# Attention scores, rough scores and broadcast maxima as 64x64 tiles, with keys stored without zero blocks

## The chip, the cores and the metric

The kernel runs on one core of a Trainium2 chip. The metric is the device time of one execution in microseconds (us), as the median of several runs. A core has TensorE (matmuls, PE in the profile; its weight loads are PEld), VectorE (DVE), ScalarE (ACT), GpSimd (POOL) and SyncE (SP), which here issues nearly all DMAs. The engines run their own instruction streams and wait for one another by semaphores.

## What is computed

The input is `x` (8 images, 128 channels, 64x64). It is cut into windows of 8x8 = 64 tokens. Only what matters for the change is shown:

```python
def mha(q, k, v, wq, wk, wv, wf, bf):
    qh = (q @ wq).reshape(B, Lq, HEADS, dh)      # 8 heads of 16
    kh = (k @ wk).reshape(B, Lk, HEADS, dh)
    vh = (v @ wv).reshape(B, Lk, HEADS, dh)
    attn = jnp.einsum('bqhd,bkhd->bhqk', qh, kh) * (1.0 / dh ** 0.5)
    attn = jax.nn.softmax(attn, axis=-1)
    o = jnp.einsum('bhqk,bkhd->bqhd', attn, vh).reshape(B, Lq, C)
    return o @ wf + bf
```

There is self-attention inside each window at 64x64, then at 16x16 after a mean over 4x4 pixels, and cross-attention in which each 64x64 window takes its keys and values from an overlapping 8x8 patch of the small map. Layernorms stand between, a feed-forward layer of 512 follows with a third layernorm, and then a 3x3 convolution of the signs of the result with the signs of its weights, batch-normalised over all images and added to its input.

## The kernel before

**Units and pairs.** The work is cut into units: a strip of 8 rows of an image (8 windows) is a `self` unit and later a `cross` unit, and the small map of an image is a `low` unit. A unit is worked in pairs of windows (4 in a strip, 2 in a small map), 528 pairs in all. Each pair goes through `rough`, `scores`, `exp`, `prob_lo` and `weigh`.

**The order.** `stages_in_order` gives each stage of each unit a due time, in pair slots: the unit's position (`at`) plus an offset from the tables `SELF`, `CROSS`, `LOW` (lines 48 to 61). Sorted, that is one list, and every engine walks it for its own stages, SyncE's queue too. For a unit at position p, the moves of its queries stand at p - 7, the key projection and its two parts at p - 6.8 to p - 6.45, the moves of the keys at p - 6, the value projection at p - 5.8, and the load of `xin` at p - 10.3. The scores of pair k stand at p + k - 1, the rough scores at p + k - 1.95, `weigh` at p + k + 0.5. The rough scores of a pair therefore come right behind the scores of the pair before it, and the scores often right behind a `weigh`.

**Queries and keys.** For accuracy queries and keys are held as a float16 high part and a float16 low part. `q_hi` (ScalarE, line 705) and `q_lo` (VectorE, line 841) write `q_flat`; `k_hi` (713) and `k_lo` (848) write `k_flat`, with the pair index innermost, so that the elements of a window are four apart. In a cross unit GpSimd's `take_keys` (1064) copies the keys from `k_image` into the same layout instead. SyncE's `move_q` (408) and `move_k` (422) then bring them, by eight DMAs each, to `qs` and `ks`, in which a head has 128 rows: 2 key parts x 2 windows x 2 query parts x 16 dimensions. Both moves wait until the scores of the last pair that used the buffer are done (line 403). In `ks` the rows of window w hold keys only in the columns of window w; the other columns are zero, set once at the start by three memsets (990). One product over 128 rows is so the sum of all four products of parts, for two windows at once.

**The three steps on TensorE per pair**, each of 8 matmuls:
- `rough_scores` (566): queries are the stationary operand (128 rows x 64 columns), keys of both windows the moving one (128 columns, stepped by four). Even heads go to PSUM partitions 0 to 63, odd heads to 64 to 127. VectorE takes the maximum of each row and writes it, negated, to `negmax` (873).
- `scores` (575): keys are stationary (128x128, stepped), queries moving (64 columns); the result stands with keys on the partitions.
- the broadcast of the maxima (580): for four pairs of heads and two windows, a column of `negmax` repeated 64 times is stationary (128x64), the identity is moving (128 columns); it adds the negated maxima to the scores.

ScalarE then takes the exponential twice (743, 744: float32 and float16), GpSimd subtracts to get the low part (1033), and `weigh` (593) multiplies with the values in 12 matmuls.

**The value projection** (536) uses the same PSUM bank `ps_proj` as the key projection, so it waits for `k_lo`.

Of the kernel before, what the change touches and what calls it, by code (L numbers as in the profile page):

```python
# [6 lines left out]
ALU = mybir.AluOpType  # L7
ACT = mybir.ActivationFunctionType
AX = mybir.AxisListType
F32 = mybir.dt.float32  # L10
F16 = mybir.dt.float16
# [4 lines left out]
TOK = WIN * WIN  # L16
HEADS = 8
# [4 lines left out]
PAIRS = SW // (2 * TOK)  # L22
# [3 lines left out]
LPAIRS = LT // (2 * TOK)  # L26
# [22 lines left out]
            v=-5.8, v_hi=-5.6, v_lo=-5.45, v_move=-5.0, turn=4.16, turned=4.24, resid=5.2, project=6.2,  # L49
# [7 lines left out]
           v=-6.6, v_hi=-6.4, v_lo=-6.25, v_move=-5.8, turn=2.38, turned=2.46, resid=3.0, project=3.2, stats=3.4,  # L57
# [49 lines left out]
def attention_conv(nc, x, wq, wk, wv, wf, bias_rows, columns, w1, w2, convw, consts, out):  # L107
# [56 lines left out]
    def pair_no(u, k):  # L164
        return u.first + k + 1

    def last_pair(u):
        return u.first + u.pairs
# [9 lines left out]
    with ExitStack() as ctx:  # L178
        def sb(name, shape, dt=F32):
            return ctx.enter_context(nc.sbuf_tensor(name, shape, dt))  # L180

        def bank(name):
            return ctx.enter_context(nc.psum_tensor(name, [128, 512], F32))

        def sem(name):
            return ctx.enter_context(nc.semaphore(name))
# [15 lines left out]
        identb = sb("identb", [128, 128], BF16)  # L202
# [10 lines left out]

        q_flat = sb("q_flat", [128, 2, 2, PAIRS * TOK], F16)

        k_flat = sb("k_flat", [128, 2, 2, TOK, PAIRS], F16)
        q_flat_low = sb("q_flat_low", [128, 2, 2, LPAIRS * TOK], F16)
        k_flat_low = sb("k_flat_low", [128, 2, 2, TOK, LPAIRS], F16)
        v_flat = sb("v_flat", [128, 2, 4 * PAIRS, VC], F16)
        v_flat_low = sb("v_flat_low", [128, 2, 4 * LPAIRS, VC], F16)  # L220

        qs = [sb(f"qs{b}", [128, HEADS, PAIRS, TOK], F16) for b in range(2)]
        qs += [sb("qs2", [128, HEADS, LPAIRS, TOK], F16)]
        ks = [sb(f"ks{b}", [128, HEADS, 2, TOK, PAIRS], F16) for b in range(2)]
        ks += [sb("ks2", [128, HEADS, 2, TOK, LPAIRS], F16)]

        vb = [sb(f"vb{b}", [128, 2, 2, 4 * PAIRS, VC], F16) for b in range(2)]
        vb += [sb("vb2", [128, 2, 2, 4 * LPAIRS, VC], F16)]
        negmax = sb("negmax", [128, 2, 8], BF16)
# [35 lines left out]
        def rows_of(t):  # L265
# [6 lines left out]
        ps_proj, ps_hid, ps_max, ps_s, ps_o, ps_t, ps_y, ps_y2 = (  # L272
            bank(n) for n in ("ps_proj", "ps_hid", "ps_max", "ps_s", "ps_o", "ps_t", "ps_y", "ps_y2"))
# [13 lines left out]
        s_k_moved = [sem(f"s_k_moved{b}") for b in range(3)]  # L287
# [8 lines left out]
        s_proj_lo = sem("s_proj_lo")  # L296
# [52 lines left out]
        def flat_q(u):  # L349
            return q_flat_low if u.kind == "low" else q_flat  # L350

        def flat_k(u):
            return k_flat_low if u.kind == "low" else k_flat
# [4 lines left out]
        def image_of(u):  # L358
            return u.no if u.kind == "low" else u.no // STRIPS
# [17 lines left out]
        def _(sp):  # L377
# [21 lines left out]
            def move_q(u):  # L399

                sp.wait_ge(s_proj_lo, proj_no["q", u.seq, None])
                if same_b[u.seq] is not None:
                    sp.wait_ge(s_s, last_pair(same_b[u.seq]))
                for a in range(2):
                    for w in range(2):
                        for b in range(2):
                            r = 64 * a + 32 * w + 16 * b
                            sp.dma_start(qs[u.b][r:r + 16, :, :, :].rearrange("d h p t -> d h (p t)"),  # L408
                                         flat_q(u)[:, w, b, :]).then_inc(s_q_moved[u.b], 16)

            def move_k(u):
                if u.kind == "cross":
                    sp.wait_ge(s_k_taken, u.no + 1)
                else:
                    sp.wait_ge(s_proj_lo, proj_no["k", u.seq, None])
                if same_b[u.seq] is not None:
                    sp.wait_ge(s_s, last_pair(same_b[u.seq]))
                for a in range(2):
                    for w in range(2):
                        for b in range(2):  # L420
                            r = 64 * a + 32 * w + 16 * b
                            sp.dma_start(ks[u.b][r:r + 16, :, w, :, :].rearrange("d h t p -> d h (t p)"),  # L422
                                         flat_k(u)[:, a, w, :, :].rearrange("c t p -> c (t p)")
                                         ).then_inc(s_k_moved[u.b], 16)

            def move_v(u):
                sp.wait_ge(s_proj_lo, proj_no["v", u.seq, None])
# [29 lines left out]
            def store_out(u):  # L457
# [4 lines left out]

            setup_bias()
            walk({"load": load, "q_move": move_q, "k_move": move_k, "v_move": move_v, "v_keep": keep_v,
                  "v_fetch": fetch_v, "store": store, "out_store": store_out})

# [36 lines left out]
        def _(pe):  # L503
            mm = nc.tensor.matmul
# [53 lines left out]
            def rough_scores(u, k):  # L558
                if k == 0:
                    pe.wait_ge(s_q_moved[u.b], 128 * moves[u.seq])  # L560
                    pe.wait_ge(s_k_moved[u.b], 128 * moves[u.seq])
                if pair_no(u, k) > 1:
                    pe.wait_ge(s_neg, pair_no(u, k) - 1)
                for h in range(HEADS):
                    j, h2 = h // 2, h % 2
                    done = mm(ps_max[64 * h2:64 * h2 + 64, 128 * j:128 * j + 128], qs[u.b][:, h, k, :],  # L566
                              ks[u.b][:, h, :, :, k].rearrange("p w t -> p (w t)"), start=True, stop=True,
                              skip_group_check=True)
                done.then_inc(s_max, 1)

            def scores(u, k):
                if pair_no(u, k) > 1:
                    pe.wait_ge(s_exp, pair_no(u, k) - 1)
                for h in range(HEADS):
                    mm(ps_s[:, TOK * h:TOK * h + TOK], ks[u.b][:, h, :, :, k].rearrange("p w t -> p (w t)"),  # L575
                       qs[u.b][:, h, k, :], start=(h == 0), stop=False, skip_group_check=True)
                pe.wait_ge(s_neg, pair_no(u, k))
                for j in range(4):
                    for win in range(2):
                        done = mm(ps_s[64 * win:64 * win + 64, 128 * j:128 * j + 128],  # L580
                                  negmax[:, pair_no(u, k) % 2, 2 * j + win:2 * j + win + 1].to_broadcast([128, TOK]),
                                  identb[:, :], start=False, stop=True, skip_group_check=True)
                done.then_inc(s_s, 1)

            def weigh(u, k):
# [110 lines left out]
        def _(act):  # L696
            activation = nc.scalar.activation
# [10 lines left out]
            def k_hi(u):  # L708
                act.wait_ge(s_proj, proj_no["k", u.seq, None])
                if before_k[u.seq] is not None:  # L710
                    act.wait_ge(s_k_moved[before_k[u.seq].b], 128 * moves[before_k[u.seq].seq])
                n = 2 * u.pairs * TOK
                activation(flat_k(u)[:, 0, :, :, :].rearrange("c w t p -> c w p t"),
                           ps_proj[:, 0:n].rearrange("c (w p t) -> c w p t", w=2, t=TOK), ACT.Identity
                           ).then_inc(s_proj_hi, 1)

            def v_hi(u):
# [117 lines left out]
        def _(dve):  # L835
            v = nc.vector
# [8 lines left out]
            def k_lo(u):  # L845
                dve.wait_ge(s_proj_hi, proj_no["k", u.seq, None])
                n = 2 * u.pairs * TOK
                v.tensor_tensor(flat_k(u)[:, 1, :, :, :].rearrange("c w t p -> c w p t"),
                                ps_proj[:, 0:n].rearrange("c (w p t) -> c w p t", w=2, t=TOK),
                                flat_k(u)[:, 0, :, :, :].rearrange("c w t p -> c w p t"), ALU.subtract  # L850
                                ).then_inc(s_proj_lo, 1)

            def v_lo(u):
                dve.wait_ge(s_proj_hi, proj_no["v", u.seq, None])
# [131 lines left out]
            v.memset(ones2[0:2, :], 1.0)  # L986
            v.tensor_tensor(brow_lo[:, :], brow_f[:, :], brow_hi[:, :], ALU.subtract).then_inc(s_prep_v, 1)

            for b in range(3):
                v.memset(ks[b][:, :, :, :, :], 0.0)  # L990
            dve.wait_ge(s_setup, 16 * len(setup_loads))
            v.tensor_copy(identb[:, :], ident[:, :]).then_inc(s_prep_v, 1)

# [25 lines left out]
        def _(pool):  # L1019
            g = nc.gpsimd  # L1020
# [37 lines left out]
            def take_keys(u):  # L1058
                pool.wait_ge(s_k_image, image_of(u) + 1)
                if before_k[u.seq] is not None:  # L1060
                    pool.wait_ge(s_k_moved[before_k[u.seq].b], 128 * moves[before_k[u.seq].seq])
                top = STRIDE * (u.no % STRIPS) * WIN
                k = k_image[:, image_of(u) % 2, :, :, :, top:top + TOK]
                g.tensor_copy(k_flat[:, :, :, :, :].rearrange("c a w t p -> c (a w) p t"),
                              k.rearrange("c a w p t -> c (a w) p t")).then_inc(s_k_taken, 1)

            g.memset(smap[:, :, :], 0.0)
# [65 lines left out]
```

## Time and profile before

| what | value |
|---|---|
| median of 3 runs | 2700.24 us (2686.36 to 2701.25) |
| the profiled execution | 2692.97 us |
| its span (first to last instruction) | 2691.2 us |
| mean granted TensorE clock | 0.933 |
| busy in the span | PE 84%, PEld 66%, DVE 61%, ACT 53%, POOL 38% |
| DMA | 288.26 MB, mean 107 GB/s |

Durations below come from the profiled execution. An instruction's duration on TensorE overlaps with its neighbours', so that what a row of matmuls costs is read from start to start. "x8" in a timeline row means eight instructions merged, from the first start to the last end.

### The profile page before, as it was taken

The numbers are of one execution on the slowest core, as the hardware profiler recorded it, in microseconds if no ns is written. First come the engines' busy times: TensorE is split into PE (matmuls) and PEld (weight loads), VectorE is DVE, ScalarE is ACT, GpSimd is POOL, SyncE is SP. The second block draws the span as 40 slices with busy tenths as digits, with TensorE's granted clock in tenths as the row PEclk, the third lists the DMA queues.
The fourth block names the chain that finished last, engine by engine and source line by source line (L and its number), as shares of the span: only waits on it lengthen the run. The fifth ranks groups of instructions, "written<-read, shape, count | busy, mean of one in ns | idle before, by whom it ended". The sixth has DMA issues, their size and how long they took to land.

```text
span 2691.2 us, 68616 instructions
## 1 busy us (share of the span) xinstructions
PE 2260.2 (84%) x27032; PEld 1774.8 (66%) x27032; DVE 1637.2 (61%) x5101; ACT 1420.7 (53%) x2531; POOL 1035.6 (38%) x1080
## 2 busy tenths in 40 slices
PE   5887878999799988999799988999799998999700
PEld 4666666777677766777677766777677766777500
DVE  4776665666466665667566665666566655545332
ACT  3654555555366655666466654565456554445332
POOL 3433434443344343444344443444344544443100
PEclk9998999999799999999899998999799999999955
DMA  4553444444244433444244433444334433323077
GB/s 104 130 125 92 122 100 103 109 111 107 75 111 110 110 96 96 109 110 113 77 112 112 109 96 87 112 107 107 82 103 110 112 94 83 80 72 82 19 234 262
DMA packets 387234, 288.26 MB, mean 107 GB/s; under 512 B 61537, under 2 KB 326498, under 8 KB 386914
## 3 DMA queue, kind: packets, MB, share of 16 engines
q1 hardware_dynamic: 386066, 282.88, 40.0%
q8 instruction: 216, 3.54, 0.6%
q14 instruction: 104, 0.85, 0.1%
q10 hardware_dynamic: 848, 0.99, 0.1%
HBM read 69.87 MB, written 56.46 MB: 47 GB/s over the span
## 4 chain that ended last, share of the span: by engine, by line
PE 56%; DVE 17%; SPq 10%; DMA 9%; issue 3%; ACT 3%; POOL 1%; POOLq 0%; ACTq 0%; DVEq 0%
PE ps_y L656 8%; SPq L408 8%; PE ps_hid L645 8%; PE ps_proj L511 6%; PE ps_o L593 5%; PE ps_max L566 4%; PE ps_s L580 4%; PE ps_hid L675 4%; PE ps_s L575 3%; DVE onorm L885 3%; PE ps_y L612 2%; PE ps_y L625 2%; DVE xn L927 2%; PE ps_t L606 2%; SPq L422 2%
## 5 line engine op out<-in xcount | busy, mean ns | idle before, releaser
L1033 POOL TENSOR_TENSOR prob_lo<-prob,prob_hi 128x512 f16<-128x512 f32 x528 | 610.9, 1157 | 931.7 <-ACT prob_hi L744 931.6
L743 ACT ACTIVATE prob<-ps_s 128x512 f32<-128x512 f32 x528 | 315.1, 597 | 403.2 <-PE ps_s L580 401.5
L873 DVE TENSOR_REDUCE negmax<-ps_max 128x8 bf16<-128x512 f32 x528 | 360.3, 682 | 155.9 <-PE ps_max L566 154.5
L880 DVE RECIPROCAL rden<-ps_o 128x8 f32<-128x8 f32 x528 | 108.0, 205 | 548.6 <-PE ps_o L593 547.4
L566 PE MATMUL ps_max<-ks,qs 128*64 128x128 f16 x4224 | 328.2, 288 | 0.3 <-issue 0.2
L885 DVE TENSOR_TENSOR onorm<-ps_o,rden 64x128 f32<-64x128 f32 x1056 | 304.8, 289 | 25.6
L744 ACT ACTIVATE prob_hi<-ps_s 128x512 f16<-128x512 f32 x528 | 313.4, 594 | 0.0
L593 PE MATMUL ps_o<-vb,prob_hi 128*128 128x68 f16 x4224 | 295.1, 197 | 1.6 <-DVE onorm L885 1.6
L656 PEld LDWEIGHTS ps_y<-w_sb,hid 128*128 128x128 f32 x2048 | 266.2, 196 | 33.3 <-issue 28.5
L645 PE MATMUL ps_hid<-xf,w_sb 128*128 128x512 f32 x512 | 283.4, 636 | 3.0 <-ACT yconv L801 2.1
L656 PE MATMUL ps_y<-w_sb,hid 128*128 128x128 f32 x2048 | 277.3, 279 | 0.6 <-ACT hid L782 0.6
L593 PEld LDWEIGHTS ps_o<-vb,prob_hi 128*128 128x128 f16 x4224 | 262.1, 100 | 11.6 <-issue 6.5
L593 PE MATMUL ps_o<-vb,prob_lo 128*128 128x68 f16 x2112 | 260.3, 197 | 0.0
L1024 POOL TENSOR_TENSOR vareps<-mv,consts_sb 128x4 f32<-128x4 f32 (+1 forms) x200 | 39.7, 199 | 545.0 <-DVE mv L900 315.6
L575 PE MATMUL ps_s<-qs,ks 128*128 128x64 f16 x4224 | 230.0, 199 | 1.2 <-ACT prob_hi L744 1.2
L580 PE MATMUL ps_s<-identb,negmax 128*64 128x128 bf16 x4224 | 225.1, 230 | 3.0 <-DVE negmax L873 2.9
L575 PEld LDWEIGHTS ps_s<-qs,ks 128*128 128x128 f16 x4224 | 207.5, 117 | 26.9 <-issue 10.6
L782 ACT ACTIVATE hid<-ps_hid,columns_sb 128x512 f32<-128x512 f32 x256 | 176.1, 688 | 86.5 <-PE ps_hid L645 85.3
L593 PEld LDWEIGHTS ps_o<-vb,prob_lo 128*128 128x128 f16 x2112 | 205.3, 100 | 24.1 <-issue 5.0
L566 PEld LDWEIGHTS ps_max<-ks,qs 128*64 128x64 f16 x4224 | 212.6, 122 | 1.2 <-issue 1.2
L755 ACT ACTIVATE oT<-ps_t 64x256 f32<-64x256 f32 (+1 forms) x544 | 202.0, 371 | 15.9 <-PE ps_t L606 7.6
L1027 POOL TENSOR_TENSOR rstd<-vareps,consts_sb 128x4 f32<-128x4 f32 (+1 forms) x200 | 198.8, 994 | 15.8
(107 smaller groups left out, 3705.3 us busy)
## 6 DMA issues: line engine op xcount, KB each, us to landing
qs<-q_flat SPq DMA_DIRECT2D x1024, 64.0 KB, 2.5
ks<-k_flat SPq DMA_DIRECT2D x1024, 64.0 KB, 2.7
vb<-v_flat SPq DMA_DIRECT2D x128, 136.0 KB, 2.4
vb<-values_out SPq DMA_DIRECT2D x128, 136.0 KB, 2.8
xin<-in_x SPq DMA_DIRECT2D x64, 256.0 KB, 3.3
self_out<-xa SPq DMA_DIRECT2D x64, 256.0 KB, 2.9
xin<-self_out SPq DMA_DIRECT2D x64, 256.0 KB, 3.3
ffn_out<-x SPq DMA_DIRECT2D x64, 256.0 KB, 2.5
```

Of the source, the lines that this page charges most:

```text
L408: sp.dma_start(qs[u.b][r:r + 16, :, :, :].rearrange("d h p t -> d h (p t)"), flat_q(u)[:, w, b, :]).then_inc(s_q_moved[u.b], 16)
L566: done = mm(ps_max[64 * h2:64 * h2 + 64, 128 * j:128 * j + 128], qs[u.b][:, h, k, :], ks[u.b][:, h, :, :, k].rearrange("p w t -> p (w t)") ...
L575: mm(ps_s[:, TOK * h:TOK * h + TOK], ks[u.b][:, h, :, :, k].rearrange("p w t -> p (w t)"), qs[u.b][:, h, k, :], start=(h == 0), stop=False ...
L580: done = mm(ps_s[64 * win:64 * win + 64, 128 * j:128 * j + 128], negmax[:, pair_no(u, k) % 2, 2 * j + win:2 * j + win + 1].to_broadcast([1 ...
L593: done = mm(ps_o[:, 2 * VC * j:2 * VC * j + 2 * VC].rearrange("p (w c) -> p w c", w=2), pp[:, pair_no(u, k) % 2, 128 * j:128 * j + 128], v ...
L645: mm(ps_hid[:, :], w1_sb[:, C * b:C * b + C], xf[:, u.no % 2, :], start=True, stop=True, skip_group_check=True).then_inc(s_hid, 1)
L656: done = mm(ps_y2[:, C * p:C * p + C], hid[:, b % 2, C * p:C * p + C], w2_sb[:, b, :], start=False, stop=(b == FB - 1), skip_group_check=True)
L743: activation(prob[:, pair_no(u, k) % 2, :], ps_s[:, :], ACT.Exp)
L744: activation(prob_hi[:, pair_no(u, k) % 2, :], ps_s[:, :], ACT.Exp).then_inc(s_exp, 1)
L873: v.tensor_reduce(negmax[:, pair_no(u, k) % 2, :], ps_max[:, :].rearrange("p (a t) -> p a t", t=TOK), AX.X, ALU.max, negate=True).then_inc ...
L885: done = v.tensor_tensor(onorm[r, u.seq % 2, k, :].rearrange("p (w j d) -> p j w d", w=2, j=4), blocks[r, :, :, DH * h2:DH * h2 + DH], r2[ ...
L1033: g.tensor_tensor(prob_lo[:, i, :], prob[:, i, :], prob_hi[:, i, :], ALU.subtract).then_inc(s_prob, 1)
```

## The change

Score rows are grouped by window: rows 0 to 63 of `qs` and `ks` now belong to window 0 and rows 64 to 127 to window 1, each with 2 key parts x 2 query parts x 16 dimensions. `ks` has no zero blocks and no window index, and the pair index is no longer innermost. The three steps work one head and one window at a time: 16 matmuls each, of 64 rows by 64 columns with 64 moving columns; window 0 uses rows and PSUM partitions 0 to 63, window 1 uses 64 to 127. The maxima of window w and head h stand in `negmax` at partition 64w + query, column h. The three memsets go. `k_hi`, `k_lo` and `take_keys` write unstepped.

```diff
-        k_flat = sb("k_flat", [128, 2, 2, TOK, PAIRS], F16)
+        k_flat = sb("k_flat", [128, 2, 2, PAIRS * TOK], F16)
...
-        ks = [sb(f"ks{b}", [128, HEADS, 2, TOK, PAIRS], F16) for b in range(2)]
-        ks += [sb("ks2", [128, HEADS, 2, TOK, LPAIRS], F16)]
+        ks = [sb(f"ks{b}", [128, HEADS, PAIRS, TOK], F16) for b in range(2)]
+        ks += [sb("ks2", [128, HEADS, LPAIRS, TOK], F16)]
...
-                            r = 64 * a + 32 * w + 16 * b
-                            sp.dma_start(ks[u.b][r:r + 16, :, w, :, :].rearrange("d h t p -> d h (t p)"),
-                                         flat_k(u)[:, a, w, :, :].rearrange("c t p -> c (t p)")
-                                         ).then_inc(s_k_moved[u.b], 16)
+                            r = 64 * w + 32 * a + 16 * b
+                            sp.dma_start(ks[u.b][r:r + 16, :, :, :].rearrange("d h p t -> d h (p t)"),
+                                         flat_k(u)[:, a, w, :]).then_inc(s_k_moved[u.b], 16)
...
                 for h in range(HEADS):
-                    j, h2 = h // 2, h % 2
-                    done = mm(ps_max[64 * h2:64 * h2 + 64, 128 * j:128 * j + 128], qs[u.b][:, h, k, :],
-                              ks[u.b][:, h, :, :, k].rearrange("p w t -> p (w t)"), start=True, stop=True,
-                              skip_group_check=True)
+                    for win in range(2):
+                        r = slice(64 * win, 64 * win + 64)
+                        done = mm(ps_max[r, TOK * h:TOK * h + TOK], qs[u.b][r, h, k, :], ks[u.b][r, h, k, :],
+                                  start=True, stop=True, skip_group_check=True)
...
                 for h in range(HEADS):
-                    mm(ps_s[:, TOK * h:TOK * h + TOK], ks[u.b][:, h, :, :, k].rearrange("p w t -> p (w t)"),
-                       qs[u.b][:, h, k, :], start=(h == 0), stop=False, skip_group_check=True)
+                    for win in range(2):
+                        r = slice(64 * win, 64 * win + 64)
+                        mm(ps_s[r, TOK * h:TOK * h + TOK], ks[u.b][r, h, k, :], qs[u.b][r, h, k, :],
+                           start=(h == 0), stop=False, skip_group_check=True)
                 pe.wait_ge(s_neg, pair_no(u, k))
-                for j in range(4):
+                for h in range(HEADS):
                     for win in range(2):
-                        done = mm(ps_s[64 * win:64 * win + 64, 128 * j:128 * j + 128],
-                                  negmax[:, pair_no(u, k) % 2, 2 * j + win:2 * j + win + 1].to_broadcast([128, TOK]),
-                                  identb[:, :], start=False, stop=True, skip_group_check=True)
+                        r = slice(64 * win, 64 * win + 64)
+                        done = mm(ps_s[r, TOK * h:TOK * h + TOK],
+                                  negmax[r, pair_no(u, k) % 2, h:h + 1].to_broadcast([64, TOK]),
+                                  identb[r, r], start=False, stop=True, skip_group_check=True)
...
-                activation(flat_k(u)[:, 0, :, :, :].rearrange("c w t p -> c w p t"),
-                           ps_proj[:, 0:n].rearrange("c (w p t) -> c w p t", w=2, t=TOK), ACT.Identity
+                activation(flat_k(u)[:, 0, :, :], ps_proj[:, 0:n].rearrange("c (w t) -> c w t", w=2), ACT.Identity
                            ).then_inc(s_proj_hi, 1)
...
-            for b in range(3):
-                v.memset(ks[b][:, :, :, :, :], 0.0)
```

`k_lo` and `take_keys` change in the same way as `k_hi`, `k_flat_low` as `k_flat`, and `move_q` numbers its rows as `move_k` does.

## Rows read from the trace of the kernel before

**Rows 1.** 290-2520 us: busy PE, PEld, DVE, ACT, POOL (instructions), PEclk, DMA share, GB/s

```profile
290.00:2520.00 2230.00, 2008.11 (x24026) 1582.01 (x24023) 1393.79 (x4503) 1225.01 (x2222) 926.59 (x958) 0.96 0.39 99
```

**Rows 2.** The waits of TensorE: us in total, times, longest us

```profile
PE ps_t L664 <- DVE xn L927: 63.1, 49, 4.5
PE ps_proj L536 <- DVE k_flat L848: 39.6, 52, 2.7
```

**Rows 3.** The chain that ended last, whole span: by engine (page), then by line

```profile
PE 56%; DVE 17%; SPq 10%; DMA 9%; issue 3%; ACT 3%; POOL 1%; POOLq 0%; ACTq 0%; DVEq 0%
...
by line: PE ps_y L656 8.1%; SPq L408 7.7%; PE ps_hid L645 7.7%; PE ps_proj L511 5.9%; PE ps_o L593 5.2%; PE ps_max L566 4.4%; PE ps_s L580 4.3%; PE ps_hid L675 3.7%; issue 3.3%; PE ps_s L575 3.2%; DVE onorm L885 2.6%; PE ps_y L612 2.3%; PE
```

**Rows 4.** The chain by line from 40 to 290 us, then pieces from 1255 us on

```profile
by line: SPq L408 22.8%; PE ps_proj L511 10.2%; SPq L422 9.1%; DMA xin<-in_x 8.6%; PE ps_s L580 4.4%; issue 4.3%; DMA ks<-k_flat 4.2%; PE ps_o L593 4.0%; PE ps_s L575 3.1%; PE ps_max L566 2.7%; ACT k_flat L713 2.7%; DVE k_flat L848 2.6%; PE
...
1255.06 0.59 SPq L408
...
1260.20 3.77 DMA xin<-in_x
...
1264.01 1.13 PE ps_proj L511 x4
```

**Rows 5.** The chain's pieces for one pair that lies on it: start us, us, what

```profile
1250.48 0.27 PE ps_s L575 x8
1250.74 0.34 PE ps_s L580 x8
1251.09 0.46 PE ps_max L566 x8
```

**Rows 6.** TensorE's order in one pair: start us, us, then the matmuls

```profile
1204.28 0.19 PE L593 MATMUL ps_o<-vb,prob_hi 128*128 128x68 f16 x1
...
1204.62 0.19 PE L593 MATMUL ps_o<-vb,prob_hi 128*128 128x68 f16 x1
1204.65 0.43 PE L575 MATMUL ps_s<-qs,ks 128*128 128x64 f16 x8
1205.01 0.41 PE L580 MATMUL ps_s<-identb,negmax 128*64 128x128 bf16 x8
1205.25 0.62 PE L566 MATMUL ps_max<-ks,qs 128*64 128x128 f16 x8
1205.81 0.70 PE L645 MATMUL ps_hid<-xf,w_sb 128*128 128x512 f32 x1
```

**Rows 7.** All instructions of a line: count, duration ns min/median/max

```profile
L566 PE MATMUL ps_max<-ks,qs x4224: 217/294/317, 32.7 to 2498.7; 128*64 128x128 f16 x192
...
L575 PE MATMUL ps_s<-qs,ks x4224: 190/198/261, 37.3 to 2505.7; 128*128 128x64 f16 x192
...
L580 PEld LDWEIGHTS ps_s<-identb,negmax x4224: 105/110/178, 37.9 to 2506.0; 128*64 128x64 bf16 x192
L580 PE MATMUL ps_s<-identb,negmax x4224: 219/219/316, 37.9 to 2506.1; 128*64 128x128 bf16 x192
```

**Rows 8.** The broadcast's opening: matmuls begun by 1205.027 us, loads begun by 1205.035 us

```profile
1205.01 0.25 PE L580 MATMUL ps_s<-identb,negmax 128*64 128x128 bf16 x2
...
1205.00 0.14 PEld L580 LDWEIGHTS ps_s<-identb,negmax 128*64 128x64 bf16 x3
```

**Rows 9.** Groups by line and form on ScalarE and VectorE: count, busy us, mean ns, idle before

```profile
L713 ACT ACTIVATE k_flat<-ps_proj 128x512 f16<-128x512 f32 x64 | 84.4, 1319 | 88.8 <-PE ps_proj L511 54.2 <-DMA ks<-k_flat 29.7 <-DMA ks<-k_flat_low 4.9
L705 ACT ACTIVATE q_flat<-ps_proj 128x512 f16<-128x512 f32 x128 | 76.3, 596 | 59.7 <-PE ps_proj L511 48.5 <-DMA qs<-q_flat_low 10.7
...
L848 DVE TENSOR_TENSOR k_flat<-ps_proj,k_flat 128x512 f16<-128x512 f32 x64 | 83.6, 1306 | 23.2 <-ACT k_flat L713 21.8
L856 DVE TENSOR_TENSOR v_flat<-ps_proj,v_flat 128x512 f16<-128x512 f32 x64 | 44.3, 692 | 7.1 <-ACT v_flat L722 5.1
```

**Rows 10.** The program's start: the last memset and the first projection

```profile
10.76 0.91 DVE L990 MEMSET ks<- 128x1024 uint32 x1 [0.16 <-issue]
...
14.82 2.04 PE L511 MATMUL ps_proj<-xin,wq_sb 128*128 128x256 f32 x4 [14.82 <-DMA xin<-in_x]
```

More of the change, by code:

```diff
@@ L214, in attention_conv @@
         q_flat = sb("q_flat", [128, 2, 2, PAIRS * TOK], F16)
-        k_flat = sb("k_flat", [128, 2, 2, TOK, PAIRS], F16)
+        k_flat = sb("k_flat", [128, 2, 2, PAIRS * TOK], F16)
         q_flat_low = sb("q_flat_low", [128, 2, 2, LPAIRS * TOK], F16)
-        k_flat_low = sb("k_flat_low", [128, 2, 2, TOK, LPAIRS], F16)
+        k_flat_low = sb("k_flat_low", [128, 2, 2, LPAIRS * TOK], F16)
         v_flat = sb("v_flat", [128, 2, 4 * PAIRS, VC], F16)
@@ L420, in move_k @@
                         for b in range(2):
-                            r = 64 * a + 32 * w + 16 * b
-                            sp.dma_start(ks[u.b][r:r + 16, :, w, :, :].rearrange("d h t p -> d h (t p)"),
-                                         flat_k(u)[:, a, w, :, :].rearrange("c t p -> c (t p)")
-                                         ).then_inc(s_k_moved[u.b], 16)
+                            r = 64 * w + 32 * a + 16 * b
+                            sp.dma_start(ks[u.b][r:r + 16, :, :, :].rearrange("d h p t -> d h (p t)"),
+                                         flat_k(u)[:, a, w, :]).then_inc(s_k_moved[u.b], 16)
             def move_v(u):
@@ L847, in k_lo @@
                 n = 2 * u.pairs * TOK
[L848 to L851, printed above, removed]
+                v.tensor_tensor(flat_k(u)[:, 1, :, :], ps_proj[:, 0:n].rearrange("c (w t) -> c w t", w=2),
+                                flat_k(u)[:, 0, :, :], ALU.subtract).then_inc(s_proj_lo, 1)
             def v_lo(u):
@@ L1063, in take_keys @@
                 k = k_image[:, image_of(u) % 2, :, :, :, top:top + TOK]
-                g.tensor_copy(k_flat[:, :, :, :, :].rearrange("c a w t p -> c (a w) p t"),
+                g.tensor_copy(k_flat[:, :, :, :].rearrange("c a w (p t) -> c (a w) p t", t=TOK),
                               k.rearrange("c a w p t -> c (a w) p t")).then_inc(s_k_taken, 1)
```

## The prediction

> **What bounds the kernel now.** I read the page's sums first, then a table by stretch, the waits of TensorE, the chain of waits, and last the order of TensorE's instructions inside one attention pair. Between 290 and 2520 us TensorE is busy 2008 of 2230 us (90%) at a granted clock of 0.96, VectorE 63%, ScalarE 55%, GpSimd 42% [rows 1]. TensorE is in front, but it is not alone. Its longest waits are for VectorE results, 63.1 us in all before the output transposes and 39.6 us before the value projection, the latter for the low part of the keys [rows 2]. The chain that ended last runs through TensorE for 56%, VectorE for 17% and SyncE's issuing plus DMA for 19% [rows 3]. The SyncE pieces are one loop: the last scores of a unit free `qs`, SyncE then issues eight query moves, each 0.6 us, the next `xin` load stands behind them, and TensorE's next projection starts as that load lands, 9.0 us after the first move's issue (1255.06 to 1264.01) [rows 4]. A faster TensorE meets this loop.
>
> How much of a TensorE saving reaches the end? The three lines of the change, 566, 580 and 575, have 4.4, 4.3 and 3.2% of the chain [rows 3]: 11.9% of 2691 us, 320 us. Had the chain passed through all 528 pairs it would hold 528 x (0.27 + 0.34 + 0.46) = 565 us [rows 5]. So 57% of the pairs lie on the chain, and I let 0.57 of a saving through. In the first stretch (40 to 290 us) SyncE's line 408 alone has 22.8% of the chain [rows 4], so little is gained there.
>
> **TensorE, before.** Within one pair [rows 6]: last matmul of `weigh` starts at 1204.62, scores at 1204.65, maxima broadcast at 1205.01, rough scores at 1205.25, next work at 1205.81. That is 0.03 + 0.36 + 0.24 + 0.56 = 1.19 us. The cadence follows from merged lengths and single durations. Scores: (430 - 198)/7 = 33 ns a matmul, weights of 128 columns read with a step of four elements [rows 6, 7]; `weigh`, unstepped, takes 31 ns (0.34 us over 11 steps) [rows 6]. Broadcast: four pairs of 128 columns in 0.24 us; the two halves of a pair start together (each lasts at least 0.219, and at the opening two lie within 0.25 us) [rows 6 to 8]. Rough scores: (620 - 294)/3 = 109 ns for each pair of the same 128 columns, about twice the broadcast's 56 (24 ns of whose 0.24 us is the first weight load). I read the doubling as the price of the stepped moving keys, whose single matmul is also 294 ns against 219 [rows 7].
> Two edges cost extra. From the last scores matmul (1204.65 + 0.23) to the broadcast's first is 0.13 us; from the last rough matmul (1205.58) to the following 128-column work 0.23 us. Both are the matmul's own duration (0.198 and 0.294) less 0.07. From broadcast to rough, both with 64 output columns, there is no such pause. So changing the tile's shape waits for the array to empty.
>
> **TensorE, after.** 24 matmuls a pair become 48, each 64 rows by 64, moving 64 columns, window 0 and window 1 in turn. Two tiles that lie diagonally can run as the two column halves do now. Let P be the time of such a pair of tiles. The leaving edge of scores goes, an entering one appears: 194 ns (`weigh`) less 70 = 0.125 us in place of 0.03. Inside there are 23 steps P. The exit is a contiguous 64-column matmul of about 198 ns less 70 = 0.13. Sum: 0.255 + 23 P.
> What is P? From below: 64 columns move in 29 ns (`weigh`'s 68 columns take 31), and the weight load must fit beside. In the broadcast's opening, three 64-column loads lie within 0.14 us when one takes 0.11, so the third, which is for the same half as the first, began some 30 ns after it [rows 7, 8]. So a 64-column load can follow another of its half in 30 ns. From above: the fastest lasting stream of instructions in these rows is 4 in 56 ns (two loads, two matmuls of the broadcast), which gives P = 56. Nearest row for a 64-column move is `weigh`: I take P = 31 ns.
> Then 0.255 + 0.713 = 0.97 us, a saving of 0.22 us a pair, 528 x 0.22 = 117 us on TensorE; the bounds are 0.27 us saved (P = 29) and 0.35 us added (P = 56). Of the 117, scores and broadcast give nothing (0.25 against 0.23 and 0.22); all comes from rough scores, by contiguous keys. 117 x 0.57 = 67 us.
> The Trainium skill, TensorE: Matmul & The Clock Gate, LDWEIGHTS section, puts a load at its columns divided by 1.2 per ns, 53 ns for 64 columns, whatever the rows; by it P would be about 56 and the sum would come out slower. The 30 ns between first and third load speak against it here.
>
> **Keys without the stepped layout.** `k_hi` on ScalarE takes 1319 ns and `k_lo` on VectorE 1306 ns, 64 times each; the same shapes without the step take 596 (`q_hi`) and 692 (`v_lo`) [rows 9]. Together 1.33 us less between key and value projection. TensorE waits there 52 times, 0.76 us on average [rows 2], so all 39.6 us can go; but the projection then meets the next thing. The bounds are 10 us (most of it found again in later waits) and 40 us; I take 28. The copy in `take_keys` gets an unstepped target too; it lies in GpSimd's idle time (42% busy [rows 1]): nothing. The moves keep their count and size, eight a unit on SyncE's queue: nothing. The three memsets end at 11.67 us while the first projection waits until 14.82 for its `xin` load, whatever VectorE does [rows 10]: nothing. The doubled instruction stream has its price in P.
>
> **Sum.** 2693.0 (the profiled execution: span 2691.2 and 1.8 around it) - 67 - 28 = 2598. The median of the runs is 7 us above the profiled one, so I give 2605.
>
> **The rivals.**
> (a) *The pairs of tiles are held to 56 ns*, by loads or by the rate of instructions. For: nothing in the rows streams faster than 14 ns per instruction for long. Against: the opening of the broadcast, three loads and two matmuls within some 30 ns [rows 8]. 0.255 + 23 x 0.056 = 1.54 us, +0.35 x 528 = +186 us on TensorE. An added cost also moves pairs onto the chain, so I let 0.7 through: +130 - 28 = +102, time 2802. The point of decision is P = 41, where TensorE's sum equals today's; past 43 the key savings are gone as well.
> (b) *The two tiles take turns*, since both write one PSUM bank. Then P = 2 x 29.5 = 59: +0.42 x 528 x 0.7 - 28 = +128, time 2828. Against: broadcasts of two column halves write one bank together now [rows 8]. For: no row has two row halves at work.
> This is the rule of the Trainium skill, TensorEngine Tiling (Array Packing), PSUM Pressure: different row tiles cannot access the same bank at the same time. No run here shows it yet.
> (c) *Half way*, P = 44: 1.27 us, +0.08 x 528 x 0.57 - 28 = -4, time 2696, no change.
> (d) *The SyncE loop takes the gain*: TensorE reaches the projection earlier and waits for `xin`. By the due times the moves of a unit are released at its position - 6 and the next unit's query projection stands at - 3.8, so the loop has 2.2 pair slots; at 4.7 us a slot (2475 us for 528 pairs) that is 10.3 us for those 9.0, so little room. If only a fifth of the 117 passes: -23 - 23 = -46, time 2654.
>
> **How the numbers follow.** Forecast 0.50, (d) 0.12, (c) 0.12, (a) 0.16, (b) 0.10. Faster by over 1% (27 us, about what a measurement of this kernel tells from no change): 0.62; within: 0.12; slower: 0.26. The low end is P = 29 with three quarters passed, 145 x 0.75 + 40 = 149, so 2551, rounded to 2550; the high end, 2800, leaves out (b) and half of (a). The forecast's own range is 2560 to 2650.
>
> **What would show it.** Right: the broadcast's first matmul about 0.25 us after the scores' first, the rough scores' 0.25 us after that; single rough matmuls near 200 ns; an entering pause of 0.125 us before the scores; `k_hi` near 600 ns, `k_lo` near 690; the wait before the value projection under 15 us; longer waits for `xin`. Wrong: 0.45 us between these starts (a, b; (b) if the two halves of a pair start 29 ns apart instead of together), or unchanged `k_hi` and `k_lo`, or a granted clock below 0.93 over the span.

## The result, and the profile after

| | before | after |
|---|---|---|
| median | 2695.63 us (13 runs, 2686.36 to 2701.67) | 2705.32 us (13 runs, 2697.09 to 2716.53) |
| profiled execution, span | 2692.97, 2691.2 us | 2705.03, 2703.2 us |

The ratio is 1.0043 [1.0027, 1.006]. The change makes the kernel 0.4% slower, 12 us by the ratio: no change by the 1% that the prediction set, but not the 88 us less that it forecast (2605 us).

TensorE did become faster. In the same stretch as [rows 1] it is busy 55 us less, at nearly the same clock, and ScalarE, VectorE and GpSimd are less busy too. Table by stretch, after (us, then busy PE, PEld, DVE, ACT, POOL, PEclk, DMA share, GB/s):

```profile
290.00:2520.00 2230.00, 1952.92 (x35297) 1553.58 (x35295) 1367.28 (x4498) 1184.31 (x2217) 835.74 (x956) 0.95 0.39 100
```

TensorE's order in one pair, after (start us, us), answers to [rows 6]:

```profile
370.21 0.20 PE L596 MATMUL ps_o<-vb,prob_hi 128*128 128x68 f16 x1
370.33 0.44 PE L577 MATMUL ps_s<-qs,ks 64*64 64x64 f16 x16
370.61 0.42 PE L583 MATMUL ps_s<-identb,negmax 64*64 64x64 bf16 x16
370.86 0.42 PE L567 MATMUL ps_max<-ks,qs 64*64 64x64 f16 x16
371.21 0.70 PE L648 MATMUL ps_hid<-xf,w_sb 128*128 128x512 f32 x1
```

From start to start: 0.12 entering, 0.28 scores, 0.25 broadcast, 0.35 rough scores and exit, 1.00 us against 1.19 before. These are also the medians of the 287 pairs that stand in this order in the two traces (1.001 and 1.193 us). The two tiles of a pair start 3 ns apart, and pairs follow one another every 31.6 ns (the broadcast's 0.253 us over eight).

Groups by line (count, busy us, mean ns, idle before), after, answer to [rows 9] and show GpSimd's copy, which took 2494 ns before:

```profile
L716 ACT ACTIVATE k_flat<-ps_proj 128x512 f16<-128x512 f32 x64 | 38.1, 596 | 99.4 <-DMA ks<-k_flat 59.4 <-PE ps_proj L511 35.5 <-DMA ks<-k_flat_low 4.4
L850 DVE TENSOR_TENSOR k_flat<-ps_proj,k_flat 128x512 f16<-128x512 f32 x64 | 44.3, 692 | 10.6 <-ACT k_flat L716 8.4
...
L1062 POOL COPY k_flat<-k_image 128x1024 f16<-128x1024 f16 x64 | 66.3, 1036 | 29.9 <-DMA ks<-k_flat 18.3 <-DMA ks<-k_flat_low 11.5
```

So every part works. The time comes back in TensorE's waits (us in total, times, longest), of which these two are of before and were small:

```profile
PE ps_proj L511 <- DMA xin<-in_x: 26.8, 14, 14.8
PE ps_proj L511 <- DMA xin<-self_out: 6.6, 13, 2.1
```

and these are of after:

```profile
PE ps_t L667 <- DVE xn L927: 65.6, 49, 4.4
PE ps_proj L511 <- DMA xin<-in_x: 57.0, 31, 14.9
PE ps_proj L511 <- DMA xin<-self_out: 41.1, 31, 2.2
...
PE ps_proj L536 <- DVE k_flat L850: 12.6, 38, 1.4
```

The wait before the value projection fell from 39.6 to 12.6 us, 27 as forecast. The waits for `xin` rose from 33 to 98 us; about 15 of each is the start of the program. 62 of the 128 loads of `xin` are now waited for, 27 before. The chain moved to the same place. By engine, after, whole span, and below it by line from 40 to 290 us, against [rows 3] and [rows 4]:

```profile
PE 45%; SPq 17%; DVE 16%; DMA 14%; issue 4%; ACT 2%; POOL 1%; POOLq 0%; ACTq 0%; DVEq 0%
```

```profile
by line: SPq L409 27.6%; DMA xin<-in_x 18.0%; PE ps_proj L511 13.6%; PE ps_o L596 4.8%; issue 4.5%; PE ps_s L577 3.9%; SPq L423 3.7%; PE ps_y L615 2.9%; PE ps_s L583 2.8%; DVE onorm L885 1.9%; PE ps_max L567 1.4%; PE ps_proj L545 1.3%; DMA 
```

SyncE's issuing and DMA had 19% of the chain before and have 31% now; TensorE fell from 56 to 45%. The part that ends last is the loop of [rows 4]: last scores of a unit, eight query moves (409), `xin` load, projection (511).

But that loop should at worst keep its own length, and the kernel got longer. The loop grew. From the first query move's issue to the landing of the `xin` load behind it, over 127 of the 128 loads in each trace, it takes 9.1 us at the median and 9.5 in the mean before, 9.4 and 10.0 after. Of the 0.47 us in the mean 0.21 lie in the issuing and 0.25 between the load's issue and its landing, whose medians the page has (before, then after):

```profile
xin<-in_x SPq DMA_DIRECT2D x64, 256.0 KB, 3.3
...
xin<-in_x SPq DMA_DIRECT2D x64, 256.0 KB, 3.5
```

What stands beside the longer issues? These are the records of SyncE's DMA issues from the first `xin` load to 2450 us, counted from the traces, beside the packets of queue q8, whose kind is "instruction" (5.16 MB in 315 packets after, 16 KB each):

```
               q8        issues                  of these, during    all issues during
               packets   all   over 0.8 us   a q8 packet         a q8 packet
before         216       2707  169           165                 295
after          315       2691  259           255                 449
```

The 99 more packets are the 25,344 more TensorE instructions (528 x 24 matmuls and as many loads), 256 to a packet. The median issue is 598 ns in both, but all issues of query and key moves together took 1403 us before and 1479 us after; the query moves and `xin` loads alone grew from 781 to 816 us. After, a query or key move's issue takes 1.08 us in the mean beside a packet and 0.60 elsewhere. One long issue, after, on SyncE's timeline, and the DMA queues around it (packets, MB, share of 16 engines):

```profile
117.00 2.25 SPq L423 DMA_DIRECT2D ks<-k_flat  x1
```

```profile
q1 hardware_dynamic: 273, 0.31, 48.1%
q8 instruction: 1, 0.02, 4.9%
```

An issue that usually takes 0.6 us takes 2.25 us, and in that stretch one instruction packet came in.

The Trainium skill, Runtime: NRT & Kernel Launch, Instruction fetch mechanics, says that instructions come in blocks of 16 KiB, 256 instructions each, through a DMA queue that the engine's sequencer drives. The packets' size and the 99 more of them agree. It calls the cost mostly hidden; 255 of 259 long issues beside a packet suggest a price on SyncE's side.

### The profile page after: what moved, and what is told of

Same layout as the page of the kernel before. It is cut to its first block, busy times and chain, and to the rows that moved or that the text cites. A ratio compares the mean times of both kernels' runs of the same rounds, so it can differ in the third digit from the quotient of the medians.

```text
span 2703.2 us, 93957 instructions
## 1 busy us (share of the span) xinstructions
PE 2204.2 (82%) x39704; PEld 1750.5 (65%) x39704; DVE 1597.8 (59%) x5098; ACT 1371.9 (51%) x2531; POOL 944.6 (35%) x1080
## 3 DMA queue, kind: packets, MB, share of 16 engines
q8 instruction: 315, 5.16, 0.9%
## 4 chain that ended last, share of the span: by engine, by line
PE 45%; SPq 17%; DVE 16%; DMA 14%; issue 4%; ACT 2%; POOL 1%; POOLq 0%; ACTq 0%; DVEq 0%
SPq L409 15%; PE ps_proj L511 7%; PE ps_y L659 7%; PE ps_hid L648 6%; DMA xin<-in_x 5%; PE ps_o L596 5%; DMA xin<-self_out 4%; PE ps_s L577 4%; DVE onorm L885 3%; PE ps_hid L678 3%; DVE xn L927 3%; PE ps_s L583 3%; PE ps_y L615 2%; DVE stats L914 2%; PE ps_max L567 2%
## 5 line engine op out<-in xcount | busy, mean ns | idle before, releaser
L659 PEld LDWEIGHTS ps_y<-w_sb,hid 128*128 128x128 f32 x2048 | 266.9, 196 | 31.6 <-issue 26.8
L511 PE MATMUL ps_proj<-xin,wq_sb 128*128 128x256 f32 x512 | 158.0, 436 | 108.3 <-DMA xin<-in_x 57.0
L577 PE MATMUL ps_s<-qs,ks 64*64 64x64 f16 x8448 | 238.5, 198 | 1.5 <-ACT prob_hi L746 1.5
L577 PEld LDWEIGHTS ps_s<-qs,ks 64*64 64x64 f16 x8448 | 179.0, 111 | 83.3 <-issue 56.5
L583 PE MATMUL ps_s<-identb,negmax 64*64 64x64 bf16 x8448 | 227.5, 196 | 3.8 <-DVE negmax L873 3.8
L567 PE MATMUL ps_max<-ks,qs 64*64 64x64 f16 x8448 | 226.8, 195 | 1.6 <-issue 1.6
```

The lines of the kernel that those rows point to most:

```text
L511: done = mm(ps_proj[:, win * n:(win + 1) * n], w, src[:, win, :, :], start=True, stop=True, skip_group_check=True)
L577: mm(ps_s[r, TOK * h:TOK * h + TOK], ks[u.b][r, h, k, :], qs[u.b][r, h, k, :], start=(h == 0), stop=False, skip_group_check=True)
L583: done = mm(ps_s[r, TOK * h:TOK * h + TOK], negmax[r, pair_no(u, k) % 2, h:h + 1].to_broadcast([64, TOK]), identb[r, r], start=False, stop ...
L659: done = mm(ps_y2[:, C * p:C * p + C], hid[:, b % 2, C * p:C * p + C], w2_sb[:, b, :], start=False, stop=(b == FB - 1), skip_group_check=True)
```

## Experiments

The theories to be told apart: the loop through SyncE takes the gain; the added instruction packets make that loop longer; TensorE loses the time in the steps themselves; tiles of 64 rows cost granted clock or time elsewhere.

**Fewer instructions with the same keys.** e1 keeps the rows and zero blocks of before and stores only the keys unstepped; scores are cut by window into halves of 64 stationary columns. It has 32 matmuls a pair.

```diff
-        ks = [sb(f"ks{b}", [128, HEADS, 2, TOK, PAIRS], F16) for b in range(2)]
+        ks = [sb(f"ks{b}", [128, HEADS, 2, PAIRS, TOK], F16) for b in range(2)]
...
-                    mm(ps_s[:, TOK * h:TOK * h + TOK], ks[u.b][:, h, :, :, k].rearrange("p w t -> p (w t)"),
-                       qs[u.b][:, h, k, :], start=(h == 0), stop=False, skip_group_check=True)
+                    for win in range(2):
+                        mm(ps_s[64 * win:64 * win + 64, TOK * h:TOK * h + TOK], ks[u.b][:, h, win, k, :],
+                           qs[u.b][:, h, k, :], start=(h == 0), stop=False, skip_group_check=True)
```

> Keys stored unstepped as in the change, but rows and zero blocks of before: scores 16 matmuls of 128 rows x 64 columns, broadcast and rough 8 each of 128x64 with 128 moving columns; 32 matmuls a pair, against 24 before and 48 in the change. By the cadences read so far TensorE needs 0.125 + 8 x 0.031 + 4 x 0.056 + 3 x 0.056 + 0.15 = 0.92 us a pair, a little less than the change's 0.97. Theory A (the change's gain is lost because the loop scores - query moves on SyncE - xin load sets the pace, and because 99 more 16 KB packets of TensorE instructions make SyncE's DMA issues longer): 33 more packets instead of 99, issue time of the moves up by some 25 us instead of 76, time below the change's by 15 to 40 us, so 2665 to 2690. Theory B (the loss belongs to the loop alone, packets don't matter): like the change, 2700 to 2710.

Measured: 2664.96 us, ratio 0.9911 [0.9885, 0.9937], at the edge of theory A's range and far from B's. Its pair, in the same view as above:

```profile
364.88 0.20 PE L593 MATMUL ps_o<-vb,prob_hi 128*128 128x68 f16 x1
365.01 0.44 PE L575 MATMUL ps_s<-qs,ks 128*64 128x64 f16 x16
365.28 0.39 PE L580 MATMUL ps_s<-identb,negmax 128*64 128x128 bf16 x8
365.51 0.39 PE L565 MATMUL ps_max<-ks,qs 128*64 128x128 f16 x8
365.83 1.12 PE L645 MATMUL ps_hid<-xf,w_sb 128*128 128x512 f32 x2
```

That is 0.95 us a pair, 0.05 less than the change, and 249 packets against 315. e2 is e1 with the rough scores and the broadcast also cut, into 16 matmuls of 64 moving columns: as many instructions as the change, but full rows.

```diff
-                for h in range(HEADS):
-                    j, h2 = h // 2, h % 2
-                    done = mm(ps_max[64 * h2:64 * h2 + 64, 128 * j:128 * j + 128], qs[u.b][:, h, k, :],
-                              ks[u.b][:, h, :, k, :], start=True, stop=True,
-                              skip_group_check=True)
+                for win in range(2):
+                    for h in range(HEADS):
+                        j, h2 = h // 2, h % 2
+                        at = 128 * j + 64 * win
+                        done = mm(ps_max[64 * h2:64 * h2 + 64, at:at + 64], qs[u.b][:, h, k, :],
+                                  ks[u.b][:, h, win, k, :], start=True, stop=True,
+                                  skip_group_check=True)
...
```

> As e1_contig, but broadcast and rough scores cut into 16 matmuls of 64 moving columns each: 48 matmuls a pair like the change, all over 128 rows in column halves, no row halves. Theory A: same cadence (31 ns a pair of tiles), same number of instruction packets and same long issues on SyncE as the change, so 2700 to 2710, 15 to 40 us above e1. Rival R (something in the 64-row tiles themselves costs time): clearly below the change. Theory B: e1 and e2 differ only by TensorE's 0.05 us a pair, at most 5 to 10 us.

Measured: 2692.39 us, 1.0011 [0.9983, 1.0039], below the range of theory A (2700 to 2710). Cutting alone costs 27 us. Its query moves and `xin` loads take 811 us to issue, e1's 786, but 26 us of the 27 could as well be 0.05 us x 528 on TensorE. The two profiled executions (2676.89 and 2658.23 us) lean that way: TensorE is busy 2186.0 us in e2 and 2162.5 in e1, 23 us more, and its waits for `xin` are 86 and 79 us, 7 more. So in these executions the loop has at most a small part in the difference.

**Taking the loop away.** The load of `xin` is placed 0.75 pair slots earlier, before the query moves in SyncE's queue, so that it no longer stands behind their wait. e3 is the change with this, e4 is before with it, e6 is e1, e7 is e2.

```diff
-SELF = dict(load=-10.3, ...
+SELF = dict(load=-11.05, ...
```

(the same in `CROSS`.)

> The change with one number altered: load at -11.05 instead of -10.3, so that the xin load stands ahead of the query moves of the unit before in SyncE's queue and no longer waits for its scores. Theory A and B: TensorE's waits for xin (98 us in the change) go to under 20 us and the time falls to about 2640 (2610 to 2665). Rival C (the loss is the lower granted clock or TensorE's own drains, the xin waits would only be replaced by others): within 10 us of the change.

> The kernel before with the same altered number. Theory A and B: only 33 us of xin waits stand there and TensorE is the bound behind, so it gains less than the change does: 2670 to 2690. So change minus before turns from +12 us to -20 us or more between these two. Rival C: the difference between the two stays at about +12 us.

> e1_contig with load at -11.05. With the loop out of the way TensorE's time counts: 0.05 us a pair less than e3_after_load_early, so 528 x 0.05 x 0.6 = 16 us below it, about 2600. Theory D (a tile of 64 rows counts as less work for the clock's gate; e3 stood 357 us at the half clock before 2520 us against 195 us in e4): only some 200 to 230 us at the half clock here and time 2585 or less. Rival E (the half clock follows TensorE's pauses alone): 300 us or more, about 2600.

> e2_contig_split with load at -11.05: matmuls and cadence of e3_after_load_early, but every tile has 128 rows. Theory D: half-clock time 200 to 230 us instead of 357, time 20 to 40 us below e3's 2617. Rival E: the same as e3 in both.

The figures of time at half clock in the last two expectations can't be compared: e3's 357 us hold the program's end, e4's 195 us don't. Counted alike, up to TensorE's last instruction, the time at the lower level (1.2 of 2.4 GHz) is 235 us before, 273 after, 239 e1, 218 e2, 232 e3, 201 e4, 204 e6, 188 e7.

| | as it is | load earlier |
|---|---|---|
| before | 2695.63 | e4 2664.91, 0.9909 [0.9882, 0.9935] |
| change | 2705.32 | e3 2616.96, 0.9726 [0.9688, 0.9764] |
| e2, 48 matmuls, full rows | 2692.39 | e7 2605.42, 0.9665 [0.963, 0.9699] |
| e1, 32 matmuls, full rows | 2664.96 | e6 2586.38, 0.9608 [0.9569, 0.9647] |

By the ratios, each against the kernel before in its own session, the same step gives 25 us before, 85 with the change, 93 in e2 and 82 in e1. With the load in its old place the change costs 12 us; with the load earlier it gains 48 (2665 to 2617; the ratios are 0.9909 and 0.9726). e4 and e7 gained somewhat more and less than was expected of them (2670 to 2690, and 20 to 40 us below e3); e3 and e6 came within 2 us of a stated range or in it. In e3 the waits for `xin` are gone but for the program's start, and the chain goes back to TensorE:

```profile
PE ps_proj L511 <- DMA xin<-in_x: 14.9, 1, 14.9
```

```profile
PE 54%; DVE 23%; SPq 10%; DMA 6%; issue 4%; ACT 3%; POOL 1%; POOLq 0%; ACTq 0%; DVEq 0%
```

This shows the first theory: the loop held the change, and taking it away lets the gain out. e6 is the best of all, 3.9% faster than before by its ratio. e3 still issues as slowly as the change (261 long issues, 315 packets), so slow issuing costs where the loop is the bound.

**Are 64-row tiles dear in themselves?** e3 was 11.5 us above e7, on runs apart. Both again, on one chip:

> The kernel of e3 (64-row tiles, xin load early), beside e13 on one chip. Theory D', restated: my half-clock times for e3, e6 and e7 took in the program's end; counted to TensorE's last instruction they are 231, 204 and 187 us. Between e3 and e7, with the same cadence, 44 us at the half clock are left, which could cost up to 22 us. Theory D' (64-row tiles let the clock fall more often): mean granted clock over all executions lower than e13's by 0.005 or more and time 8 to 20 us above it. Rival (scatter between chips): clock and time within 0.002 and 5 us of e13's.

> The kernel of e7 (the same cadence and number of instructions, all tiles with 128 rows), beside e12. Theory D': about 2600, clock above e12's by 0.005 or more. Rival: as e12.

Measured: 2614.89 (0.9717 [0.9689, 0.9744]) and 2612.55 (0.9702 [0.9673, 0.9731]). They are 2 us apart and their intervals overlap, so the 8 to 20 us of theory D' did not show. But the rival did not come true either: the mean granted clock over the executions is 0.930 against 0.934, not within 0.002. The same lean stands in every couple with like cadence and like number of matmuls, 64-row tiles against full rows:

| | median us | mean granted clock | us at 1.2 GHz | busy TensorE, us |
|---|---|---|---|---|
| change, e2 | 2705.32, 2692.39 | 0.924, 0.930 | 273, 218 | 2204, 2186 |
| e3, e7 | 2616.96, 2605.42 | 0.933, 0.936 | 232, 188 | 2180, 2163 |
| e12, e13 | 2614.89, 2612.55 | 0.930, 0.934 | 236, 204 | 2178, 2165 |

(The first two columns are over all executions, the last two of the profiled one.) So a cost of 64-row tiles through a lower clock is not excluded; it is small, 2 to 13 us by the medians, and no run shows its cause. Part of the 13 us between the change and e2, whose intervals just overlap, can be this; the rest stays open.

**The price of the loop.** One more DMA of 64 KB, to an output scratch, stands behind the eight query moves: a known lengthening of the loop and of nothing else of size. e10 in the change, e11 in before.

```diff
+                sp.dma_start(extra_out[u.seq, :, :], ident[:, :]).then_inc(s_extra, 16)
```

> The change with one more DMA (128 partitions x 512 B, from the identity to a scratch array in DRAM) behind the eight query moves of each unit, ahead of the xin load: 136 issues of 0.6 to 0.7 us, some 90 us of SyncE in the loop. It prices a microsecond of SyncE's issuing. Theory A: half or more of it shows, 2703 + 45 to 90 = 2750 to 2790. Rival (issue time on SyncE is hidden): under +15.

> The same DMA in the kernel before, where TensorE and the loop were about equally long. Theory A: a smaller share shows, 2693 + 20 to 60 = 2715 to 2755. Rival: under +15.

Measured: e10 2760.17 us, 1.026 [1.0215, 1.0305]; e11 2736.4 us, 1.0171 [1.0127, 1.0216]. Both lie in the range expected. Taken from the ratios, the extra 87.5 us of issuing (136 issues) costs the change (1.026 - 1.0043) x 2693 = 58 us, 0.67 us for each; before pays 46 us for 85.2, 0.54 for each. With four executions each the intervals leave 0.5 to 0.8 and 0.4 to 0.7, so that the two prices are not told apart. Waits of e10:

```profile
PE ps_proj L515 <- DMA xin<-in_x: 83.0, 44, 14.8
...
PE ps_proj L515 <- DMA xin<-self_out: 52.5, 34, 2.5
```

They are 37 us above those of the change: the added issues arrive at TensorE. About two thirds of a lengthening of the loop is paid in the change, and about half already before. So the 35 us by which the issues of query moves and `xin` loads grew (781 to 816) are worth about 35 x 0.67 = 23 us, an estimate. The whole loop grew by more, 127 x 0.47 = 59 us with the later landing, at that price some 40 us.

**Packets without matmuls.** To add instruction packets and nothing else, waits on an event long past were placed on TensorE behind its slow stages. e5 is e1 with them, e8 has twice as many, e9 is e8's waits in e6.

```diff
+            def pad(n):
+                for _ in range(n):
+                    pe.wait_ge(s_brow, 16 * 2 * PAIRS)
```

> e1_contig with some 17,000 waits on a semaphore that was reached long before (8 to 32 behind each slow float32 or convolution stage of TensorE), so that TensorE's instruction stream has as many packets as e2_contig_split's and the change's (315), while its matmuls are e1's. Theory A (each packet holds up a DMA issue of SyncE, and the loop hands that on): issues on SyncE add up to about 1800 us as in e2, time about 2690. Rival (e2 lost against e1 by its 0.05 us more of TensorE a pair): issues may grow, but the time stays at e1's 2665.

> e5_contig_pads with twice as many spent waits: e5 came out with only 33 packets more than e1 (two waits make one instruction) and its time rose from 0.991 to 0.996 of before. Now 66 more packets, as in e2_contig_split, with e1's matmuls. Theory A (packets of TensorE instructions lengthen the loop through SyncE): about 1.000 of before (0.997 to 1.004), the added time to be found in TensorE's waits for xin. Rival (packets don't matter; e5's rise was scatter): 0.991.

> The same waits in e6_contig_load_early, where the xin load no longer stands behind the query moves. Theory A: packets cost little where the loop doesn't set the pace, 0.961 to 0.966 of before (e6: 0.961). Rival (the waits slow TensorE itself): the same rise as from e1 to e8, 0.970.

Measured: e5 2684.36 us, 0.9962 [0.994, 0.9985], 19 us above e1. Only 33 packets came in addition (282), since two waits go into one instruction, and the loop's issue time rose from 786 to 796 us only. e8: 3099.8 us, 1.1529 [1.1485, 1.1572]; e9, without the loop: 3075.64, 1.1435 [1.1397, 1.1474]. That is 435 us above e1 and 489 above e6, and the waits of e8 say why:

```profile
PE ps_o L599 <- issue: 203.4, 338, 1.4
PE ps_s L581 <- issue: 72.8, 60, 1.6
```

All waits of this kind, in which the profile shows nothing that TensorE waited for, come to 375 us in e8 and 1 us in e1; I read them as TensorE's sequencer working through the spent waits. e8 missed its expectation, and e9 showed the same rise where the loop is gone, so these two measure the waits. e5 is different: it has 0.6 us of this kind, and its waits for `xin` are 98.5 us against e1's 78.7. That is where the theory of the packets puts the rise, but the profiled execution of e5 was 5 us above its median and that of e1 7 below, and the query moves and `xin` loads took only 10 us more to issue, so it supports the theory and does not show it. e8 speaks against the simple form: with 316 packets, as many as the change, it has 202 issues over 0.8 us in the whole run, e1 204 with 249 packets, the change 271. So the number of packets alone does not make issues long; when they come must matter, or something else that comes with them. The theory stays open.

## Why the prediction was wrong

**Right, step by step.** P was taken as 31 ns and is 31.6; the tiles in one bank run together, 3 ns apart, so (a), (b) and (c) are out. The edges are 126 ns entering and 123 leaving (medians), as "duration less 70" gave (125 and 130). Rough scores carry the gain, and `k_hi` and `k_lo` take 596 and 692 ns, as their rows without the step did. The wait before the value projection gave 27 us, forecast 28. The start did not move. The Trainium skill's two rules weighed in the prediction, on loads in TensorE: Matmul & The Clock Gate, LDWEIGHTS, and on banks in TensorEngine Tiling (Array Packing), PSUM Pressure, would by the prediction's estimates have had P near 56 or 59; the 31.6 ns and the 3 ns of this trace disagree with both.

**Mis-sized.** "0.255 + 0.713 = 0.97 us, a saving of 0.22 us a pair, 117 us" measured 1.00 us, 0.19 and 101 us at the full clock: the first step within the scores takes 52 ns and not 31. TensorE's busy time over the whole span fell by only 56 us (2260.2 to 2204.2). The 37 us more at half the clock stand for some 19 us of the difference, an estimate; the rest is not attributed. The prediction also added 7 us for the median of three runs over the profiled one; with 13 runs it is 2.7 us above. In its low end 0.27 us x 528 is 142 us, not 145, which changes nothing.

**Failed 1: "I let 0.57 of a saving through."** The share of the chain says where the end was set before, not how far TensorE can shrink until another path sets it. Here the loop through SyncE, the second path, was about as long: the prediction worked out 10.3 us of slots for a loop of 9.0 us, called it little room, and still gave it a chance of 0.12. The 9.0 was one loop; the mean of 127 was 9.5. With 0.19 us less a pair the same 2.2 slots are 9.9 us, an estimate, and the loop's mean after is 10.0: no room is left. With the loop in place the change's 101 + 27 us gave -12 (profiled executions). With it out of the way they gave 48 (e4 to e3), a share of 0.37, and e4 to e6, with 0.24 us less a pair, gave 79, about a half. So even the rest of the kernel, with VectorE at 23% of e3's chain, does not let 0.57 through. The 28 us for the keys were let through whole; no run has them alone.

**Failed 2: "The moves keep their count and size, eight a unit on SyncE's queue: nothing", and "The doubled instruction stream has its price in P."** The moves' issuing took 1479 us in place of 1403, and the `xin` load landed later. In the trace the long issues lie beside packets, 255 of 259, and 99 more packets go with 90 more long issues. At the price that e10 shows, the growth in issuing is worth 23 us, more than the 12 that the change lost. Rival (d) had the mechanism and forecast 2654, since it let a fifth of the gain pass and kept the loop's length. The link from packets to long issues is read from overlap in time; no run isolates it, e5 supports it and e8 has the packets without more long issues. What made the loop longer stays open.

**Failed 3: the clock.** The granted clock fell: a mean of 0.924 over the executions of the change against about 0.935 of before, 273 us at 1.2 GHz in place of 235. "A granted clock below 0.93 over the span" was one of the prediction's own signs of being wrong. In all four kernels the clock is higher where the waits for `xin` are gone: before 0.935 and 0.938 (e4), the change 0.924 and 0.933 (e3), e1 0.926 and 0.935 (e6), e2 0.930 and 0.936 (e7). So most of the fall goes with the waits and is a part of their price; what is left between e3 and e4 may go with the 64-row tiles. The sum had no term for either.

The account for the profiled executions, 12 us in all: TensorE is busy 56 us less, and idle 72 us more up to its last instruction; what follows that is 4 us shorter. Of the 72, the waits for `xin` are 65 more and all waits for the keys' low part (`k_flat`, L850) 31 less; the rest is spread over smaller waits, of which those for `onorm` (10 us), `xf` (8) and `xn` (6) grew most. A binding loop of unchanged length would give about zero; for the 12 us above that stand the longer loop and the lower clock, and how much is due to which was not separated.

## What to carry to other kernels

Before a saving on the busiest engine is credited, work out the length of the next longest loop and compare the two; take its mean over many units and not one piece of it, and shrink the room by the saving itself. Where there is about a microsecond of room in ten, the loop can take the whole gain, and the cheapest repair may be one line: a load that stands behind a blocking wait in its queue goes ahead of it (e3, e4, e6). Prefer the form that gets the same streaming with fewer instructions: unstepped keys with 128 moving columns (e1, e6) took all of the gain with 32 matmuls a pair in place of 48. Instructions are traffic too: each 256 on TensorE were one more 16 KB transfer here, and nearly all long DMA issues lay beside one, though no run shows that they are the cause.

## What I had not expected of the hardware

- A DMA issue on SyncE, 598 ns at the median, takes over 0.8 us in 165 of the 295 cases in which an instruction packet is under way before, and in 255 of 449 after. Outside of packets only 4 of 2242 are so long after.
- A moving operand stepped by four float16 elements halves the rate, as guessed from two rows: e1, with the rough scores' shape kept and only the step gone, took 0.32 us for them and the exit where before took 0.56, and two column halves followed one another every 56 ns where before they took 115 (medians). Before it was a reading of two lines; here it is the one thing changed in that step.
- Waits on TensorE that are long satisfied are not free in number: some 17,000 instructions of them in e8 cost 435 us, while half as many in e5 came with 19 us.
